# Cross-attention steps of a decoder layer reordered, and the best two gates of a tile found within its step

## The reference, cut to what matters

```python
# x: (2, 1024, 256), context: (2, 77, 256), 16 heads
x = x + attn(layernorm(x))                     # 16 heads of 64, 1/distance^2 weights, gate, W_out
# cross-attention, heads of 16
q = layernorm(x) @ Wq.T + bq ; k = ctx @ Wk.T + bk ; v = ctx @ Wv.T + bv
p = softmax(q k^T / 4 + mask * -1e9)           # 77 keys
x = x + (p v) @ Wo.T + bo
# mixture of 8 experts, 2 per token
y = rmsnorm(layernorm(x)) * rms_w              # inside: x_n + sum over the two experts
vals, idx = top_k(y @ gate_w.T, 2) ; w = softmax(vals)
x = x + x_n + sum_k w_k * W3[idx_k](silu(W1[idx_k] y) * (W2[idx_k] y))
```

## Time and profile before

| what | value |
|---|---|
| time, median of 3 runs | 1596.91 us (1594.95 to 1597.11) |
| the profiled execution, its own time | 1595.71 us |
| its span in the profile | 1593.9 us |
| TensorE matmuls busy | 1420.5 us, 89% |
| VectorE busy | 1032.5 us, 65% |
| ScalarE busy | 928.3 us, 58% |
| GpSimd busy | 650.6 us, 41% |
| mean granted TensorE clock | 0.962 |

### The profile page before, as it was taken

One profiled execution on the slowest core, in us unless ns is written; L12 is line 12 of the kernel. 1 busy time (PEld: TensorE's weight loads), 2 busy tenths in 40 slices (PEclk: granted clock), 3 DMA queues, 4 the chain that ended last, 5 costly groups with the idle time before them and its releaser, 6 DMA issues. The chain is left out here.

```text
span 1593.9 us, 23093 instructions
## 1 busy us (share of the span) xinstructions
PE 1420.5 (89%) x7425; PEld 902.2 (57%) x7426; DVE 1032.5 (65%) x1359; ACT 928.3 (58%) x646; POOL 650.6 (41%) x484
## 2 busy tenths in 40 slices
PE   6899999999999999999997568888983799999996
PEld 4555555555555555555454257777773566666664
DVE  7878988898889888988887635555566321221221
ACT  1779888988898889888989412222221122222221
POOL 5255456545654565456532612122120233333331
PEclk9999999999999999999999779999995899999998
DMA  4000000000000000000000312111120034233312
GB/s 144 14 1 14 27 26 13 13 26 26 13 13 26 26 13 13 26 27 13 7 13 14 112 57 97 39 52 40 46 81 13 21 85 138 33 84 84 87 28 71
DMA packets 67484, 66.91 MB, mean 42 GB/s; under 512 B 5152, under 2 KB 59936, under 8 KB 67424
## 3 DMA queue, kind: packets, MB, share of 16 engines
q1 hardware_dynamic: 60160, 56.58, 10.9%
q0 software_dynamic: 7296, 9.97, 3.7%
HBM read 48.70 MB, written 19.92 MB: 43 GB/s over the span
## 5 line engine op out<-in xcount | busy, mean ns | idle before, releaser
L1612 POOL TENSOR_TENSOR v_aug<-v_aug,wts 128x1024 f32<-128x1024 f32 x96 | 254.4, 2650 | 249.2 <-ACT wts L1465 244.6
L983 DVE TENSOR_SCALAR wts<-ps_s,k 128x1024 f32<-128x1024 f32 x240 | 297.1, 1279 | 86.3 <-PE ps_s L537 66.0
L1457 ACT ACTIVATE wts<-wts 128x4096 f32<-128x4096 f32 (+1 forms) x80 | 231.8, 2935 | 88.0 <-DVE wts L983 66.8
L552 PE MATMUL ps_o<-wts,g_r 128*64 128x512 f32 x1024 | 252.6, 616 | 12.7 <-ACT wts L1465 12.5
L1463 ACT ACTIVATE wts<-wts,eps_d 128x4096 f32<-128x4096 f32 (+1 forms) x80 | 241.6, 3019 | 0.2
L1465 ACT ACTIVATE wts<-wts 128x4096 f32<-128x4096 f32 (+1 forms) x80 | 235.2, 2940 | 2.5
L1378 DVE TENSOR_TENSOR wts<-rinv,ps_s 128x352 f32<-128x352 f32 x76 | 39.6, 521 | 254.5 <-ACT rinv L1530 171.3
L778 PE MATMUL ps_s<-wts,qk 128*128 x608 | 198.6, 470 | 3.2 <-issue 2.3
L972 DVE TENSOR_TENSOR v_aug<-v_aug,wts 128x1024 f32<-128x1024 f32 x96 | 156.1, 1626 | 5.4 <-ACT wts L1465 5.1
L537 PE MATMUL ps_s<-q_hi,k_hi 64*128 64x512 f32 x512 | 115.8, 446 | 41.2 <-DVE wts L983 31.1
L778 PEld LDWEIGHTS ps_s<-wts,qk 128*128 128x128 f32 x608 | 110.8, 192 | 65.2 <-issue 17.5
(11 more groups left out here) (238 smaller groups left out, 2411.7 us busy)
## 6 DMA issues: line engine op xcount, KB each, us to landing
wts<-in_w SPq DMA_DIRECT2D x16, 704.0 KB, 5.5
h_t<-o_raw SPq DMA_DIRECT2D x16, 512.0 KB, 2.7
qk<-h_t SPq DMA_DIRECT2D x16, 512.0 KB, 4.0
wts<-in_w SPq DMA_DIRECT2D x8, 640.0 KB, 7.1
raw_qk<-in_w_in SPq DMA_DIRECT2D x32, 128.0 KB, 2.2
raw_vg<-in_w_in SPq DMA_DIRECT2D x32, 128.0 KB, 2.2
acc<-wts SPq DMA_DIRECT2D x17, 128.0 KB, 1.8
wts<-in_x SPq DMA_DIRECT2D x2, 1024.0 KB, 5.9
```

The lines of the kernel that those rows point to most:

```text
L552: mm = pe.matmul(ps_o[r, t], v_pair[:, b, r], wts[:, h, b, t], start=b == 0, stop=b == SB - 1)
L983: dve.tensor_scalar(wts[:, h, b, :], ps_s[:, h, :], k2[:, 2 * b + h:2 * b + h + 1], 0.0, ALU.add, ALU.max).then_inc(S_.max_ok, 1)
L1457: act.activation(chunk(start, end), chunk(start, end), ACT.Sqrt).then_inc(S_.sqrt_ok, 1)
L1612: pool.tensor_tensor(acc_w[:, 0], acc_w[:, 0], wts[:, 0, b], ALU.add).then_inc(S_.add_ok, 1)
```

## The change

TensorE's step: only turns 0 and 1 stand ahead of `turn_x`; turns 2 and 3 follow the first product and the first two heads. The values wait for each of the four copies where its heads begin, instead of for all of them at once. `query` moves behind the second pair of heads' values, `logits` behind the third product instead of the fourth. The last products come with two or three heads each, and product 7 stands behind `turn_y`, just ahead of `turn_o`.

VectorE's step: `copy_xt` moves ahead of the copy of turn 3. A new function `best_two` at the step's end copies the gates of tile t-3 to `gl`, takes their 8 largest, copies them to `top`, searches their places and casts the first two to `top_f`. It has two new semaphores, `max8_ok` and `at_ok`, and three small tiles. The loops over 16 tiles behind the last step are gone; a memset and the cast of `sums` move between steps 16 and 17, and the weights' three operations move behind the addition to `a17`.

```diff
--- before.py
+++ after.py
@@ -180,7 +180,8 @@
         y_tile = rinv[:, 0:D].rearrange("p (c t) -> p c t", t=P)
         gl = sb("gl", [P, NT, E])
         top = sb("top", [P, NT, 8])
-        top_i = sb("top_i", [P, NT, 8], U32)
+        g_now, v_now = sb("g_now", [P, E]), sb("v_now", [P, 8])
+        at_now = sb("at_now", [P, 8], U32)
         top_f = sb("top_f", [P, NT, 2])
         pw = sb("pw", [P, 5, NT])
         w_full = sb("w_full", [P, 2, NT, E])
@@ -677,9 +678,10 @@
                 if h0 == 0:
                     if n >= 1:
                         pe.wait_ge(S_.x2_ok, i)
-                    pe.wait_ge(S_.pta_ok, 2 * i + 2)
-                    pe.wait_ge(S_.ptd_ok, 2 * i + 2)
                 for h in range(h0, h1):
+                    if h % HPB == 0:
+                        k = h // HPB
+                        pe.wait_ge((S_.pta_ok, S_.ptd_ok)[k % 2], 2 * i + k // 2 + 1)
                     mm = pe.matmul(bank_x[:, h * (XD + 1):(h + 1) * (XD + 1)], p_t[:, h, :],
                                    v_x[:, bass.ds((i >> 3) & 1, 1), h, :], start=True, stop=True)
                 if h1 == XH:
@@ -713,22 +715,35 @@
 
             def step(t, n, s1=True, s2=True, s3=True, s4=True):
 
+                def woven(q, h0, h1):
+                    if s1:
+                        attn_out(t, q, q + 1, n)
+                    if s3:
+                        x_values(t - 2, h0, h1, n - 2)
+
                 if s3:
-                    for k in range(4):
-                        turn_p(t - 2, k, n - 2)
+                    turn_p(t - 2, 0, n - 2)
+                    turn_p(t - 2, 1, n - 2)
                 if s2:
                     turn_x(t - 1, n - 1)
-                for j in range(H // 2):
-                    if s1:
-                        attn_out(t, j, j + 1, n)
-                    if s2 and j == 1:
-                        query(t - 1)
-                    if s2 and j == 3:
-                        logits(t - 1, n - 1)
-                    if s3:
-                        x_values(t - 2, 2 * j, 2 * j + 2, n - 2)
+                woven(0, 0, 2)
+                if s3:
+                    turn_p(t - 2, 2, n - 2)
+                    turn_p(t - 2, 3, n - 2)
+                woven(1, 2, 4)
+                if s2:
+                    query(t - 1)
+                woven(2, 4, 6)
+                if s2:
+                    logits(t - 1, n - 1)
+                woven(3, 6, 8)
+                woven(4, 8, 10)
+                woven(5, 10, 13)
+                woven(6, 13, 16)
                 if s4:
                     turn_y(t - 3, s2)
+                if s1:
+                    attn_out(t, 7, 8, n)
                 if s3:
                     turn_o(t - 2)
                 if s4:
@@ -1192,17 +1207,27 @@
 
             def copy_gates(i):
                 dve.wait_ge(S_.gl_mm, i + 1)
-                dve.tensor_copy(gl[:, bass.ds(i, 1), :].rearrange("p a e -> p (a e)"), bank_b[:, 0:E]).then_inc(S_.gl_ok, 1)
+                dve.tensor_copy(g_now[:], bank_b[:, 0:E]).then_inc(S_.gl_ok, 1)
+
+            def best_two(i):
+                dve.wait_ge(S_.gl_ok, i + 1)
+                dve.tensor_copy(gl[:, bass.ds(i, 1), :].rearrange("p a e -> p (a e)"), g_now[:])
+                dve.max(v_now[:], g_now[:]).then_inc(S_.max8_ok, 1)
+                dve.wait_ge(S_.max8_ok, i + 1)
+                dve.tensor_copy(top[:, bass.ds(i, 1), :].rearrange("p a e -> p (a e)"), v_now[:]).then_inc(S_.top_ok, 1)
+                dve.max_index(at_now[:], v_now[:], g_now[:]).then_inc(S_.at_ok, 1)
+                dve.wait_ge(S_.at_ok, i + 1)
+                dve.tensor_copy(top_f[:, bass.ds(i, 1), :].rearrange("p a e -> p (a e)"), at_now[:, 0:2]).then_inc(S_.topf_ok, 1)
 
             def step(t, n, s1=True, s2=True, s3=True, s4=True):
                 if s3:
                     probs_t(t - 2, 1, n - 2)
                 if s4:
                     norm_x2(t - 3, n - 3)
+                if s2:
+                    copy_xt(t - 1)
                 if s3:
                     probs_t(t - 2, 3, n - 2)
-                if s2:
-                    copy_xt(t - 1)
                 if s4:
                     expert_in(t - 3, n - 3)
                 if s2:
@@ -1225,6 +1250,8 @@
                     norm_x(t, n)
                 if s3:
                     moments2(t - 2)
+                if s4:
+                    best_two(t - 3)
 
             for t in range(4):
                 step(t, t, s2=t >= 1, s3=t >= 2, s4=t >= 3)
@@ -1235,35 +1262,26 @@
                 step(t, 4)
             for t in range(NT, NT + 3):
                 step(t, 4, s1=False, s2=t <= NT, s3=t <= NT + 1)
-
-
-            dve.wait_ge(S_.gl_ok, NT)
-            for i in range(NT):
-                q = dve.max(top[:, i, :], gl[:, i, :])
-            q.then_inc(S_.top_ok, 1)
-            dve.wait_ge(S_.top_ok, 1)
+                if t == NT:
+                    dve.memset(a17[:, NT], 0.0)
+                    dve.wait_ge(S_.rc_in, 16)
+                    dve.tensor_copy(sums, rc[:, R_TRI:R_ONES + P])
+
+            dve.wait_ge(S_.top_ok, NT)
             dve.tensor_tensor(pw[:, 0], top[:, :, 1], top[:, :, 0], ALU.subtract).then_inc(S_.dlt_ok, 1)
-            for i in range(NT):
-                q = dve.max_index(top_i[:, i, :], top[:, i, :], gl[:, i, :])
-            q.then_inc(S_.topi_ok, 1)
-            dve.wait_ge(S_.topi_ok, 1)
-            dve.tensor_copy(top_f[:], top_i[:, :, 0:2]).then_inc(S_.topf_ok, 1)
+            dve.wait_ge(S_.topf_ok, NT)
+            for k in range(2):
+                q = dve.tensor_tensor(w_full[:, k], cst[:, C_IOTA:C_IOTA + E].unsqueeze(1).broadcast_to([P, NT, E]),
+                                      top_f[:, :, k:k + 1].broadcast_to([P, NT, E]), ALU.is_equal)
+            q.then_inc(S_.oh_ok, 1)
+            dve.wait_ge(S_.oh_ok, 1)
+            dve.tensor_tensor(a17[:, 0:NT], w_full[:, 0], w_full[:, 1], ALU.add).then_inc(S_.a_ok, 1)
             dve.wait_ge(S_.pe_ok, 1)
             dve.tensor_scalar(pw[:, 2], pw[:, 1], 1.0, None, ALU.add).then_inc(S_.pw_ok, 1)
             dve.wait_ge(S_.pw_ok, 1)
             dve.reciprocal(pw[:, 3], pw[:, 2]).then_inc(S_.pw_ok, 1)
             dve.wait_ge(S_.pw_ok, 2)
             dve.tensor_tensor(pw[:, 4], pw[:, 3], pw[:, 1], ALU.mult).then_inc(S_.pw_ok, 1)
-            dve.wait_ge(S_.topf_ok, 1)
-            for k in range(2):
-                q = dve.tensor_tensor(w_full[:, k], cst[:, C_IOTA:C_IOTA + E].unsqueeze(1).broadcast_to([P, NT, E]),
-                                      top_f[:, :, k:k + 1].broadcast_to([P, NT, E]), ALU.is_equal)
-            q.then_inc(S_.oh_ok, 1)
-            dve.wait_ge(S_.oh_ok, 1)
-            dve.memset(a17[:, NT], 0.0)
-            dve.wait_ge(S_.rc_in, 16)
-            dve.tensor_copy(sums, rc[:, R_TRI:R_ONES + P])
-            dve.tensor_tensor(a17[:, 0:NT], w_full[:, 0], w_full[:, 1], ALU.add).then_inc(S_.a_ok, 1)
             dve.wait_ge(S_.rc_in, 16)
             dve.wait_ge(S_.rank_mm, 1)
```

More of the change, by code:

```diff
@@ L248, in program @@
         tok_now = sb("tok_now", [P, 2], U32)
-        names = ("x_in", "xb_in", "cst_in", "c_in", "fill_s", "fill_ok", "xnb_ok", "stats_ok", "aggr_ok", "std_ok", "rstd_ok", "xn_ok", "tr_ok", "xnt_ok",
+        names = ("x_in", "xb_in", "cst_in", "c_in", "fill_s", "fill_ok", "xnb_ok", "max8_ok", "at_ok", "stats_ok", "aggr_ok", "std_ok", "rstd_ok", "xn_ok", "tr_ok", "xnt_ok",
                  "qk_in", "vg_in", "wqk_ok", "wvg_ok", "xh_ok", "x2_in", "q_proj", "k_proj", "v_proj", "g_proj", "norm_mm", "k2_mm",
```

## The result

The changed kernel takes 1581.03 us (median of 4 executions, 1577.93 to 1582.67), the kernel before 1596.62 us (4 executions, 1594.95 to 1597.11), timed beside it. The ratio is 0.9902, with a 95% interval of 0.9884 to 0.9919: 15.6 us faster. The forecast was 1589.0, with a range of 1582 to 1595, so the kernel is just outside, on the fast side. The profiled execution took 1582.67 us, with a span of 1580.8.

What follows compares the result with a forecast made beforehand. The prediction took the circle turn_p, logits, mask, maximum, subtraction, exp to set the looped step. Loop 3.0, steps ahead 1.5, steps behind 0 and router 3.5 sum to 8.0 us: 1596.9-8.0 = 1588.9, rounded 1589, range 1582 to 1595.

Steps and rivals of the forecast that it cites:

- the circle: Looped step: turn_p to logits 7.89 us, logits 2.24, then mask, maximum, subtraction, exp to next turn_p 7.17; claimed to set the step.
- best_two 1.42 for 1.35: VectorE, between moments2 and its first copy: best_two taken to cost 1.35 us, bounds 0.6 and 1.6.
- the load 4.51 for 4.6: Load of h_tile: 4.6 us from the last product's result to the tile, a new stall of 0.4 before product 0.
- turn 3 at T+3.64 for 3.8: TensorE, T being turn_p's start: turn 3 waits for VectorE's first copy until T+3.8, a new stall of about 0.4 us.
- From q_t to the logits: TensorE, register work between the wait for q_t and the first logits matmul: 0.7 us taken, bounds 0.05 and 0.95.
- norm_x came at T+1.12 instead of 1.33: VectorE's norm_x, needed by turn_x, ends 1.33 us after turn_p's start; a new stall of 0.46 at turn_x.
- T+7.64: Logits start 7.64 us after turn_p's start instead of 7.89: step 17.05 against 17.30, 3.0 us over twelve looped steps.
- The first (best_two cheap, 1579 to 1583): Rival: best_two 0.6, register work 0.3, only the load holds up the front; steps 16.2 to 16.6 us; chance 0.18.
- The second, that the loop gains nothing: Rival: only the router and the unrolled steps gain; 1592 us, from 1590.5 to 1594; chance 0.2.
- The third, the load as the bound: Rival: load of h_tile sets the step, kernel slower; landing of 5.5 us gives step 18.1 and 1602 us; chance 0.12.
- The unrolled steps: Two steps ahead of the loop gain 1.5 us, bounds 0 and 2; three behind it nothing, bounds 1 either way.
- the router: Router's start behind the last gate copy, 5.51 us before, 2.0 left for the last tile: gain 3.5, bounds 3.0 and 3.8.

## Why the prediction was wrong

**The step that failed** is the one that names the circle: "A step gets shorter only if the logits come earlier after turn_p. What is saved behind the logits only lengthens the wait for exp." It was drawn from a wait at turn_p and a sum around exp that closes at 17.30. But a sum that closes over one period shows only that the work follows on; it closes over any path that comes back a step later. Taking 0.4 us and more out of that path changed nothing (17.31, and 16.69 after), and a product moved behind turn_y, well behind the logits, was worth 0.44.

**What the gain of 0.62 is made of**, along the circle that does bind. Ahead of turn 3 VectorE's way grew by 1.41, best_two. On TensorE's way from turn 3 to the next gates 2.03 went: product 0, turn_x and two heads stand ahead of turn 3 now (-1.02), the wait before the first values (-0.68), most of the wait before turn_o (0.71 to 0.19, -0.52), and the new wait for q_t behind the query (+0.21). These are differences of starts between the two traces, but for the +0.21, which is the row `issue`; 0.02 of the 2.03, made of small differences either way, stays open. The forecast saw each of these edits and priced nearly all of them as a stall of TensorE ahead of the logits. On the real circle product 0 and turn_x aren't stalls but cover: they lie beside best_two.

**The sizes** were close: best_two 1.42 for 1.35; the load 4.51 for 4.6; turn 3 at T+3.64 for 3.8. From q_t to the logits 0.35 lie, where 0.7 was taken, and norm_x came at T+1.12 instead of 1.33, so the logits started at T+7.08 instead of T+7.64. With 7.08 and its own 9.41 behind the logits, the forecast's rule would have given 16.49, not far from 16.69 and yet no support for the rule: without the subtraction the same step takes the same 16.69. So the forecast's number fell short by the terms ahead of the logits, the 0.7 above all. With them right it would have had 0.81 a step instead of 0.25, nearer to the measured 0.62, but by a path that doesn't set the step. The first copy's 1.87 behind moments2 lies between the 1.2 and 2.2 beyond which the forecast called best_two mis-priced.

**The Trainium skill's estimate** for best_two, by the fixed latency of small operations (VectorE: DVE Perf Modes, section on the SBUF-source errata), was 0.35. In the same section the Trainium skill says that this row of its table under-predicts a single operation. Measured are 1.42. In the trace each of the operations but one is 0.14 to 0.17 long; the copy to `top` is 0.59 in the loop and 0.17 in the unrolled steps, and an operation that waits for the result of another starts 0.29 behind it. The fit of the Trainium skill (DMA: Bandwidth & Descriptors, the fit for a transfer's time), from which the forecast had its 3.2 for the load, is given there for transfers that GpSimd issues. SyncE issues this load, and it landed in 3.9 to 4.1 in the loop after.

**The rivals.** The first (best_two cheap, 1579 to 1583) had the time right, 1581.03, and by luck: best_two was not cheap, and the step of 16.69 was not the load's. The second, that the loop gains nothing, is refuted by the steps. The third, the load as the bound, is refuted by the split load's 16.69 in the changed kernel; the load's circle came up, at 16.23, only when best_two was out of the way.

**The unrolled steps and the router** came near the forecast: -1.9 for -1.5 ahead of the loop, -3.7 for -3.5 behind the last gates. The last three steps got 1.0 longer instead of 0. In the kernel after the clock was at half from 1184.6 on, 14 us into them; in the kernel before from 1192.0 on, 12 us into them, but full again between 1198.8 and 1202.2. What part of the 1.0 is the clock and what the order was not separated.

## What to carry to other kernels

A wait in front of an instruction doesn't show that its releaser sets the period of a pipelined loop: something further down may wait just as long, as turns 2 and 3 did. Read the chain of waits over one whole period, write down each path that closes on itself, and test the one you believe in by taking a piece out of it. Work added to a step costs what the binding circle has no cover for: the same best_two cost 1.31, 0.33 or nothing, by what stood beside it. And the circle that binds changes with each edit: here it was VectorE's (16.69), then the load's (16.26), then VectorE's by norm_x (15.78), and at last that through exp (15.61).

## What the runs showed of the hardware

The granted clock moved the time of this stage more than several of the edits did. In the last three steps TensorE's matmuls fill some three quarters of the time, and the clock falls to half (1.2 GHz of 2.4) at some point of them in every run, but not at the same point. The stretch from turn_p of step 16 to the last gate copy, in the kernel before:

```profile
1180.40:1215.40 35.00, 26.84 (x144) 22.20 (x144) 16.15 (x40) 8.30 (x26) 5.15 (x5) 0.71 0.07 23
```

In the kernel with best_two late and the load in halves, and in the changed kernel without the subtraction:

```profile
1157.60:1188.50 30.90, 23.43 (x144) 19.15 (x144) 18.19 (x60) 8.27 (x25) 5.15 (x5) 0.81 0.08 26
```

```profile
1171.40:1212.90 41.50, 34.72 (x145) 29.58 (x143) 18.72 (x61) 8.39 (x25) 2.89 (x4) 0.55 0.06 19
```

The same matmuls (144 and 145 are recorded) take 30.9 us at a mean clock of 0.81 and 41.5 at 0.55. This is how a kernel that does less work came out slower in its profiled execution, the slowest of its four: without the subtraction the clock was at half from 1175.4 on, 4 us into the stretch, and two of its looped steps took 18.20 and 18.13. The fastest two kernels are equal, although one has the shorter step, in the same way: 15.61 with 35.2 us in these steps at a clock of 0.65, against 15.78 with 30.9 at 0.81. Each kernel shows a pattern of its own; what sets it these runs don't tell, and no experiment here was made for it. A median difference of 2 to 5 us between two orders of this stage should be read only beside the clock, and one between the two profiled executions beside the times of the others.
